# DRAM slots for the relative shift of the position scores, 256 KB further apart in an attention and expert kernel

## The reference

```python
def _relative_shift(x):
    b, h, s, _ = x.shape
    x = jnp.pad(x, ((0, 0), (0, 0), (0, 0), (1, 0)))
    x = x.reshape(b, h, s + 1, s)
    return x[:, :, 1:, :].reshape(b, h, s, s)
...
content_score = jnp.einsum('bhsp,bhtp->bhst', q + u, k)
pos_score = _relative_shift(jnp.einsum('bhsp,htp->bhst', q + v, pos))
score = (content_score + pos_score) / jnp.sqrt(jnp.float32(P))
out = jnp.einsum('bhst,bhtp->bhsp', jax.nn.softmax(score, axis=-1), val)
```

## Time and profile before

| what | us |
|---|---|
| median of 3 runs | 4691.83 (4685.78 to 4698.15) |
| the profiled execution | 4698.8 |
| its span, first to last instruction | 4697.0 |
| PE busy in the span | 4317.0 (92%) |
| DVE busy | 3394.8 (72%) |
| ACT busy | 3201.7 (68%) |
| POOL busy | 1263.8 (27%) |
| hardware DMA queue, share of 16 engines | 74.1% |

### The profile page before, as it was taken

One profiled execution on the slowest core, in us unless ns is written; L12 is line 12 of the kernel. 1 busy time (PEld: TensorE's weight loads), 2 busy tenths in 40 slices (PEclk: granted clock), 3 DMA queues, 4 the chain that ended last, 5 costly groups with the idle time before them and its releaser, 6 DMA issues. The chain is left out here.

```text
span 4697.0 us, 121317 instructions
## 1 busy us (share of the span) xinstructions
PE 4317.0 (92%) x48308; PEld 3333.7 (71%) x48308; DVE 3394.8 (72%) x8088; ACT 3201.7 (68%) x4124; POOL 1263.8 (27%) x905
## 2 busy tenths in 40 slices
PE   7899999999989999989998998889999999999997
PEld 3466666666666666666666666668888888888886
DVE  7688888888888888888888787755665666544455
ACT  2588888888888888888888888744444444444454
POOL 0111111111111111111111111125556666544443
PEclk9899999999999999999999999989999999999998
DMA  8999999999999999999999999972555555433259
GB/s 320 342 379 389 394 386 393 388 384 392 389 389 384 388 396 389 388 396 382 390 389 387 391 393 388 360 253 53 133 137 124 136 125 136 107 56 87 47 171 313
DMA packets 467836, 1391.15 MB, mean 296 GB/s; under 512 B 59216, under 2 KB 136656, under 8 KB 467024
## 3 DMA queue, kind: packets, MB, share of 16 engines
q1 hardware_dynamic: 418128, 1316.25, 74.1%
q0 software_dynamic: 49152, 67.14, 8.4%
HBM read 708.93 MB, written 674.23 MB: 294 GB/s over the span
## 5 line engine op out<-in xcount | busy, mean ns | idle before, releaser
L765 DVE CUSTOM_DVE_ANT_0 att_shifted<-att_quad,att_shifted 128x512 f32<-128x512 f32 x2048 | 1351.8, 686 | 507.4 <-PE att_quad L991 256.2
L604 ACT ACTIVATE ring<-att_quad 128x1024 f32<-128x1024 f32 x1024 | 1050.5, 1026 | 229.9 <-PE att_quad L980 205.2
L612 ACT ACTIVATE att_pt<-att_tp 128x1024 f32<-128x1024 f32 x1024 | 1047.7, 1023 | 17.9 <-PE att_tp L1013 13.0
L772 DVE TENSOR_SCALAR att_shifted<-att_shifted,att_mn 128x512 f32<-128x512 f32 x2048 | 1024.6, 542 | 0.0
L991 PE MATMUL att_quad<-att_kd,att_qd 64*128 64x512 f32 x2048 | 879.8, 462 | 149.2 <-DVE att_mn L765 134.6
L980 PE MATMUL att_quad<-att_pos,att_qd 64*128 64x512 f32 x2048 | 849.8, 445 | 91.4 <-ACT ring L604 84.1
L1420 ACT ACTIVATE ffn_hp<-ffn_up 128x512 fp32r<-128x512 f32 x512 | 306.2, 598 | 855.4 <-PE ffn_up L1601 818.4
L1506 DVE TENSOR_TENSOR ffn_hp<-ring,ffn_hp 128x512 fp32r<-128x512 f32 x512 | 440.4, 860 | 589.4 <-ACT ring L1422 528.8
L1012 PEld LDWEIGHTS att_tp<-ident,att_shifted 64*128 64x128 f32 x8192 | 669.6, 141 | 189.2 <-DVE att_shifted L772 109.9
L1601 PE MATMUL ffn_up<-ffn_xp,ffn_w1p 128*128 128x512 f32 x3072 | 796.1, 395 | 2.8 <-DVE ffn_xp L1449 2.8
L1012 PE MATMUL att_tp<-ident,att_shifted 64*128 64x64 f32 x8192 | 754.8, 229 | 43.1 <-ACT att_pt L612 32.8
(11 more groups left out here) (132 smaller groups left out, 5249.9 us busy)
## 6 DMA issues: line engine op xcount, KB each, us to landing
xs_d<-ring SPq DMA_DIRECT2D x1024, 513.0 KB, 8.7
att_shifted<-xs_d SPq DMA_DIRECT2D x1024, 512.0 KB, 8.8
att_shifted<-in_L_attn_x_dram SPq DMA_DIRECT2D x32, 512.0 KB, 6.6
xn_d<-att_shifted SPq DMA_DIRECT2D x32, 512.0 KB, 5.9
xt_d<-att_shifted SPq DMA_DIRECT2D x32, 512.0 KB, 7.2
gathered<-xt_d SPq DMA_DIRECT2D x32, 512.0 KB, 10.0
att_d<-att_osb SPq DMA_DIRECT2D x512, 32.0 KB
ring<-in_L_ffn_w_dram SPq DMA_DIRECT2D x16, 1024.0 KB
```

The costliest lines, as they stand in the source:

```text
L604: act.activation(xo[:, kk % NW, 2 * half:2 * half + 2, 1:S + 1], xp[:, :, :], ACT.Copy).then_inc(x_out, 1)
L612: act.activation(turned_keys(n, half), tp[:, :, :].rearrange("p r (k n) -> p k r n", k=2 * TT), ACT.Exp, scale=-1.0).then_inc(t_out, 1)
L765: dve.tensor_tensor_reduce(out=shifted[:, kk % NX, t], in0=sp_[:, t % 2], in1=shifted[:, kk % NX, t], scale=-0.25, scalar=-NEG, op0=ALU.ad ...
L772: dve.tensor_scalar(shifted[:, kk % NX, t], shifted[:, kk % NX, t], mn[:, kk % NX, t:t + 1], None, ALU.subtract).then_inc(lowered, 1)
```

## The change

The slots of `xs_d` are no longer back to back. Their pitch grows from S * (S + 1) to S * (S + 1) + S * P numbers, from 1,050,624 to 1,312,768 bytes; the numbers between two slots are not used. The tensor grows by 2 MB. Two slots that were 2,101,248 bytes apart are 2,625,536 bytes apart. Slot numbers, the order of all instructions, and the shape and size of every transfer stay as they are.

```diff
-    xs_d = nc.dram_tensor("xs_d", [S * P + 8 * S * (S + 1)], F32).ap()[S * P:].rearrange("(k n) -> k n", k=8)
+    apart = S * (S + 1) + S * P
+    xs_d = nc.dram_tensor("xs_d", [S * P + 8 * apart], F32).ap()[S * P:].rearrange("(k n) -> k n", k=8)[:, 0:S * (S + 1)]
```

## The result

The changed kernel took 4816.2 us (median of 4 runs, 4801.9 to 4829.0) against 4688.8 us before (4 runs): ratio 1.0266, 95% interval 1.0250 to 1.0282. It is slower by 127 us; 4691 us and no change had been forecast. The profiled execution is the shortest of the four, so its span shows 103 us of these: 4800.1 against 4697.0.

What follows compares the result with a forecast made beforehand. DMA throughput was taken to bound each head in the slot stretch, with PE close behind. The terms summed to 0 + 0 + 0 = 0 us, so 4691 us in terms of the median, range 4651 to 4722.

Steps and rivals of the forecast that it cites:

- the stores' dips: DMA rate drops once in four heads, after the small output stores; expected to stay, 0 counted, 168 us if all vanished.
- part 1: Slot transfers: written and read slot move from 2 MB + 4 KB to 2.504 MB apart; priced at 0 us.
- rival C: Slot write and read collide at the new distances, slower: 47 us, about 4739 us, 4715 for half; chance 0.17.
- the far end: Outer limit of a loss over the slot stretch, every four heads like the worst at 360 GB/s: 216 us more.
- one extra 3 us window per four heads: Assumed added slow window at 361 GB/s in the slot stretch, the source of the 47 us loss.
- A: Old slot distance costs a little steadily and the new one frees it: up to 41 us less, about 4651; chance 0.16.
- B: Head output stores collide with slot transfers, moved slots meet them less often: 70 us less, about 4621; chance 0.07.
- D: Program addresses are scattered in physical memory, so the slots' move does nothing: 4691 us; inside no change's 0.58.

Runs made afterwards that it cites:

- e1_tail: Kernel before the change, slots unmoved, 2 MB added at the end of xs_d so that only later tensors move: 4693.0 us, ratio 0.9995.
- e5: Kernel before the change with slot pitch 2050 KB, written and read slot 4.004 MB apart, slots still about 256 KB above 1 MB multiples: 4695.3 us, ratio 1.0011.
- e2_turned: Changed kernel with slot s placed where slot (s + 4) mod 8 lay, distances between write and read kept: 4742.5 us, 1.0101 of the kernel before.
- e11: Changed kernel writing rows 8192 bytes apart, without the column of zeroes and the relative shift: 4648.3 us, 0.9910 of the kernel before.
- e10: Kernel before the change writing rows 8192 bytes apart, without the column of zeroes and the relative shift: 4664.5 us, ratio 0.9946.

## Why the prediction was wrong

**Right.** That the DMA engines' throughput sets the head, with no slack: a rate 3.6% lower made the stretch 3.6% longer, and everything outside it kept its time (from the last slot read's issue to the end of the span 4697.0 - 3047.2 = 1649.8 us before, 4800.1 - 3151.5 = 1648.6 after). That a loss would pass through one to one, that the stores' dips stay, that the footprint costs nothing (`e1_tail`), and that distance as such is worth next to nothing (`e5`, 8 us).

**The step that failed** is part 1, "The distance". I read the change as its description has it, as a change of the distance between the slot written and the slot read, priced that at 0, and let the sentence "All low address bits, up to 256 KB, stay as they were" stand as a reason for safety. Bits that matter lie above: where a slot begins, first of all within its 1 MB. The old pitch of 1026 KB put all eight slots 256 to 270 KB above a multiple of 1 MB of the tensor, in the fast part of the curve. A pitch of 1282 KB puts them at about 256, 512, 768 and 0 KB in turn. Both numbers could be worked out from the diff. What the runs put in the place of the 0 is 127 us in the change and 46 in `e2_turned`, with the same places in the same order; with rows of 8192 bytes they put a gain of 16 us there. So it is shown that moved places cost time here when rows of 8208 bytes are written, and that the distance doesn't. How much a layout costs is not explained: slots 3 and 7 both begin just above a multiple of 1 MB (6 and 14 KB), and only the second shows the large loss; rings with the same places within 1 MB differed by up to 0.9 us per head; and `e2_turned` lost a third of the change. The curve could not be read from the trace before, for no slot stood anywhere else in it.

**The evidence that misled.** The clean 409 to 413 GB/s of the earlier trace rows showed that the old layout ran free. I used it as if it said that layouts run free. And against rival C I set the other traffic, "with arbitrary distances", that ran at 415 to 420 GB/s; that traffic has no rows of 8208 bytes, and it was the rows that counted.

**The rivals.** C had the sign and half of the mechanism: reads slowed at certain slots, by places and not by work. It was wrong on the pair (the read's place makes no difference), and its price, 47 us with 216 as the far end, against 127. My range was cut at 4722 by giving C half its price, where the sum's own rows reached 216 us: the term was mis-sized too, because one extra 3 us window per four heads was an invented amount. A is refuted for these rows, since at twice the distance (`e5`) nothing was gained; the 16 us of `e11` against `e10` are too few for its price of 41 and have no explanation. B did occur in small: after the stores at slot 1 the read packets' excess fell from 54 to 7 ns in the worst quarter, while at slot 5 it rose from 106 to 132, and both drown in the loss at slots 7 and 0. D forecast no change and is refuted by the result, and that addresses in the program matter is plain from 1 KB of base, which moves the whole kernel by 7%; that the placement in memory plays a part beside them isn't excluded.

## What to carry to other kernels

Where DMA engines are full, the addresses of a DRAM buffer are a part of the kernel's speed, and a clean rate at one layout says nothing of the next; before a layout is moved for one reason, list for each buffer what else moves (its start, the distance of its rows, what lies between them), and let a run with only the transfers, in many layouts, map it: one run of 4.6 ms with 26 layouts showed what no single whole-kernel run could. It ranks layouts, but a loss in microseconds must still be measured in the kernel. Written rows 8208 bytes apart, 16 over a power of two, were worth avoiding here, or their base worth tuning to the KB: as bases for the old pitch 256 and 512 KB were good, 257 and 513 the slowest tried. Compare layouts that differ in one thing: distance and place were separated only by a layout that doubled the one and kept the other, and by two that did the reverse.

## What the runs showed of the hardware that was not expected

- Writes in 4104-byte pieces, rows 8208 bytes apart, took from 2.9 to 10.7 us per 1 MB slot by where the slot begins, much alike from one MB to the next where a slot is written alone (4.51 to 4.74 at four multiples of 1 MB); with rows of 8192, 8256 or 9216 bytes 2.64 to 2.82 at every place tried.
- Where reads run beside slow writes, the packets that show it are not the writes' own: a read packet's mean rose to 535 ns, a write's only to 185. In writes alone it does show, up to 412 ns.
- The page DMA: Bandwidth & Descriptors of the Trainium skill (section on latency and other measured facts) warns of per-partition pitches at large powers of two and advises padding. Its pitches begin at 512 KiB; here, at 8 KB, the exact power of two was even and the one padded by 16 bytes was slow. No run here tests its own cases. The prediction held this pitch, a distance between partitions of one transfer, against the distance between two slots, which is another quantity; the distance between partitions is 8208 bytes here, before and after the change.
- A ring's time was not the same in two programs at the same place in the tensor: 5.37 and 5.57 us per head for the changed layout, 5.43 and 5.64 for the old pitch from 1024 KB, 6.37 and 6.63 from 1792, but 5.20 both times for the layout of before. The two ran on different chips. Where a tensor lies in the chip's memory isn't seen in the trace, and this was not followed up; the 127 us of the change against 46 of `e2_turned` may have the same source.
